# Expert lists visited in fixed blocks of 128 rows, with a short table for the rest

## What is computed

```python
scores = sigmoid(x @ gate_weight.T); sc = scores + gate_bias
# best 2 of 4 groups, then the best 6 of their experts
_, topidx = top_k(where(emask > 0, sc, -inf), 6)
tw = take_along_axis(scores, topidx); tw = tw / (tw.sum() + 1e-20) * 0.2
routed = sum over the 6 chosen e of tw[e] * (silu(x @ w_gate[e]) * (x @ w_up[e])) @ w_down[e]
anchor = the same with one of 16 smaller experts: topidx[:, 0] // 2
out = routed + shared + 0.1 * anchor
```

## Time and profile before

| | us |
|---|---|
| median of 3 runs (421.95 to 535.0) | 422.62 |
| span of the profiled execution | 412.1 |
| around the span, if that execution is like the median | 10.5 |
| last slots written | 178.8 |
| first visit's rows turned on TensorE | 203.14 |
| first routed up-product | 240.53 |

### The profile page before, as it was taken

The page is one execution under the profiler, slowest core; times in us unless marked ns, Lnnn a source line. Parts: engine busy times, 40 slices in busy tenths (PEclk is TensorE's granted clock), DMA queues, the critical chain, the costliest instruction groups (busy, mean ns, idle before and its releaser), DMA issues.

```text
span 412.1 us, 8817 instructions
## 1 busy us (share of the span) xinstructions
PE 343.3 (83%) x2552; PEld 299.1 (73%) x2552; DVE 278.0 (67%) x1171; ACT 190.0 (46%) x471; POOL 181.7 (44%) x159
## 2 busy tenths in 40 slices
PE   5999999999899968773889999999999999994000
PEld 3786978779687857561677789999999999993000
DVE  0466789989798886798357775555565665666675
ACT  1152153441545233400157777777877777771000
POOL 6000000588888768767871374344422344433000
PEclk9999999999999997985989999999999999998555
DMA  7999999986698643694555576555555559531998
GB/s 234 298 335 335 329 341 328 420 320 119 123 337 252 126 96 86 218 387 137 152 162 130 167 214 180 162 158 165 165 145 162 166 155 291 168 113 58 303 303 245
DMA packets 55823, 88.44 MB, mean 215 GB/s; under 512 B 16145, under 2 KB 46521, under 8 KB 55513
## 3 DMA queue, kind: packets, MB, share of 16 engines
q1 hardware_dynamic: 38192, 67.66, 52.9%
q0 software_dynamic: 16720, 19.48, 17.8%
q10 hardware_dynamic: 864, 0.73, 0.6%
HBM read 50.62 MB, written 37.09 MB: 213 GB/s over the span
## 4 chain that ended last, share of the span: by engine, by line
PE 60%; DVE 20%; DMA 8%; issue 3%; ACT 3%; SPq 3%; DVEq 2%; POOLq 0%
PE B L823 20%; PE B L838 10%; PE B L514 6%; PE B L812 5%; DMA W<-sums_d 4%; PE B L549 4%; PE B L632 3%; PE B L598 2%; PE B L618 2%; DVEq L319 2%; DMA e_sb<-rows_d 2%; SPq L419 2%; DVE ring L1589 1%; PE B L656 1%; DMA W<-in_pt 1%
## 5 line engine op out<-in xcount | busy, mean ns | idle before, releaser
L457 POOL DMA_INDIRECT rows_d<-spent,slot x77 | 104.1, 1352 | 97.3 <-issue 90.9
L823 PEld LDWEIGHTS B<-e_sb,UPW 128*128 128x128 f32 x796 | 105.4, 193 | 10.7 <-issue 5.5
L823 PE MATMUL B<-e_sb,UPW 128*128 128x128 f32 x796 | 108.9, 278 | 1.5 <-issue 1.5
L1597 DVE TENSOR_TENSOR e_sb<-e_sb,B 128x128 f32<-128x128 f32 (+1 forms) x112 | 32.3, 288 | 62.2 <-ACT e_sb L990 55.8
L981 ACT COPY UPW<-W 128x512 f32 (+1 forms) x112 | 63.9, 570 | 22.2 <-issue 13.9
L838 PE MATMUL B<-W,e_sb 128*128 x224 | 69.3, 391 | 0.8 <-DVE e_sb L1597 0.8
L483 POOL DMA_INDIRECT sums_d<-spent x32 | 31.1, 972 | 48.7 <-DVE spent L1589 47.9
L812 PE MATMUL B<-ident,e_sb 128*128 128x128 f32 x224 | 43.1, 274 | 1.9 <-DMA e_sb<-rows_d 1.8
L990 ACT ACTIVATE e_sb<-B 128x128 f32<-128x128 f32 (+1 forms) x112 | 30.9, 276 | 22.2 <-PE B L823 20.8
L514 PE MATMUL B<-W 128*111 128x256 f32 (+1 forms) x132 | 34.2, 406 | 4.6 <-DMA W<-in_pt 4.5
L483 POOL DMA_INDIRECT sums_d<-W,tok_full x24 | 23.2, 966 | 30.3 <-ACT W L995 29.7
(11 more groups left out here) (250 smaller groups left out, 524.0 us busy)
## 6 DMA issues: line engine op xcount, KB each, us to landing
e_sb<-rows_d SPq DMA_DIRECT2D x112, 161.0 KB, 2.3
rows_d<-spent SPq DMA_DIRECT2D x2, 7728.0 KB, 44.4
W<-in_wx SPq DMA_DIRECT2D x1, 6643.0 KB
W<-sums_d SPq DMA_DIRECT2D x13, 448.0 KB, 9.4
W<-in_wx SPq DMA_DIRECT2D x10, 516.5 KB, 9.5
W<-in_wx SPq DMA_DIRECT2D x1, 4576.0 KB, 18.7
W<-in_pt SPq DMA_DIRECT2D x4, 666.0 KB, 6.9
W<-sums_d SPq DMA_DIRECT2D x7, 336.0 KB, 11.1
```

Of the source, the lines that this page charges most:

```text
L457: pool.indirect_dma_start(rows_d, bass.IndirectOffsetOnAxis(ap=slot[0:n, t, j:j + 1], axis=0), xrow[0:n, t, :], None).then_inc(done, 16)
L823: mm = pe.matmul(B[2 + i % 2][:, m * P:(m + 1) * P], UPW[:, i % 2, at:at + P], GT[:, i % 2, k, :], start=k == 0, stop=k == KC - 1)
L1597: dve.tensor_tensor(out[0:n, i % 2, :], S[0:n, i % 2, :], ups, ALU.mult).then_inc(H_ok, 1)
```

## The change

There are again 112 visits, of four kinds: `a`, the first 128 rows of each of the 16 anchor lists; `b`, 9 further blocks of anchor lists; `r`, the first 128 rows of each of the 32 routed lists; `s`, 55 further blocks. For `a` and `r` the row offset, the weights and the weight column are constants, so nothing is read from the table and the gate and up weights are multiplied straight from `W`. For `b` and `s` a table of 64 places holds the weights' offset, the row and the column; a place without a block points to dummy rows. Further blocks are counted from a list's end, so only first blocks are partly filled; their unused rows go to spare rows of `sums_d` (`keep`, `spare`). No tile is summed in SBUF: each visit's weighted result goes to one of 22 buffers and is sent alone, 112 indirect DMAs; ScalarE weighs every second `a` visit, VectorE the others. All turned copies are ScalarE's. Only the first 128 rows of the lists are filled in advance. SP's queue and TensorE no longer wait for the table ahead of the first visit. At the end of the first part `route` comes ahead of `shared_down(2)`, `shared_down(3)` ahead of the table, `shared_mult(3)` ahead of the last `choose`; the product for the masks (`slot_bounds`) and some filler products (`stay_busy`) are gone.

```diff
--- before.py
+++ after.py
...
+ANCHOR_MORE = (TOKENS - 1) // P
+ROUTED_MORE = (TOKENS * TOPK - TOPK) // P
+KINDS = "a" * ANCHORS + "b" * ANCHOR_MORE + "r" * EXPERTS + "s" * ROUTED_MORE
 XT = len(KINDS)
 INDEX = [KINDS[:i].count(k) for i, k in enumerate(KINDS)]
-TILE_AXIS, EXTRA_AXIS = 1000, 2000
-RING = D + 1
+FIRST_ROUTED = ANCHORS + ANCHOR_MORE
+MORE = ANCHOR_MORE + ROUTED_MORE
+ROUTED_AXIS = 1000
 GB = 6
-PL = 3 * EXPERTS + ANCHORS
+NY, NY_OWN = 22, 10
...
+def weighed_by_act(i):
+    return KINDS[i] == "a" and i % 2 == 1
...
+        def up_place(i):
+
+            return ANCHOR_COLS + INDEX[i] * WX if routed(i) else INDEX[i] * ANCHOR_WX
+
+        def result(i):
+
+            u = i % NY
+            return Y_own[:, u * D:(u + 1) * D] if u < NY_OWN else spent[:, (u - NY_OWN) * D:(u - NY_OWN + 1) * D]
+
+        def free_result(engine, i):
+
+            if NY_OWN <= i < NY:
+                engine.wait_ge(hs_ok, NB)
+            if i >= NY:
+                engine.wait_ge(y_sent[i % NY], 16 * (i // NY))
...
-            for half in range(2):
-                sp.dma_start(of_list[half * P:(half + 1) * P, :, :],
-                             padrow[:, :].unsqueeze(1).to_broadcast([P, LISTS, ROW])).then_inc(empty, 16)
+            of_list = rows_d[P:P + LISTS * LIST_ROWS, :].rearrange("(l r) n -> r l n", r=LIST_ROWS)
+            sp.dma_start(of_list[0:P, :, :], padrow[:, :].unsqueeze(1).to_broadcast([P, LISTS, ROW])).then_inc(empty, 16)
...
             sp.wait_ge(scat_anchor, 16 * NT)
             sp.wait_ge(ini_d, 16 * 4)
-            sp.wait_ge(table_ok, 1)
             sp.wait_ge(av_ps, NT)
 
             def load_rows(i):
+                if i == ANCHORS:
+                    sp.wait_ge(table_ok, 1)
                 if i == FIRST_ROUTED:
                     sp.wait_ge(scat, 16 * NT * TOPK)
                 if i >= GB:
 
                     sp.wait_ge(T_ps, i - GB + 1)
                     sp.wait_ge(meta_ok, i - GB + 1)
-                row = entry(mybir.EngineType.SP, 1, i, DUMMY_ROW + P)
-                sp.dma_start(G[:, i % GB, :], rows_d[bass.ds(row, P), :]).then_inc(g_ld[i % GB], 16)
+                if looked_up(i):
+                    row = entry(mybir.EngineType.SP, 1, i, DUMMY_ROW + P)
+                    rows = rows_d[bass.ds(row, P), :]
+                else:
+                    row = P + (INDEX[i] + (0 if routed(i) else EXPERTS)) * LIST_ROWS
+                    rows = rows_d[row:row + P, :]
+                sp.dma_start(G[:, i % GB, :], rows).then_inc(g_ld[i % GB], 16)
...
                 if i == XT - 16:
-                    sp.wait_ge(sent_anchor, 16 * ANCHOR_PACKED)
-                    sp.wait_ge(sent_full, 16 * FULL)
+                    for u in range(NY):
+                        sp.wait_ge(y_sent[u], 16 * sends_of(u, FIRST_ROUTED))
                     load_part(TOPK)
             sp.wait_ge(D_ps, XT)
-            sp.wait_ge(sent_mixed, 16 * MIXED)
+            for u in range(NY):
+                sp.wait_ge(y_sent[u], 16 * sends_of(u, XT))
...
-            pool.wait_ge(hs_ok, NB)
-            pool.memset(spent[:, 0:until_scattered], 0.0).then_inc(mixed_zero, 1)
-            pool.wait_ge(scat_anchor, 16 * NT)
-            pool.wait_ge(scat, 16 * NT * TOPK)
             pool.wait_ge(ini_d, 16 * 4)
-            pool.memset(spent[:, until_scattered:MIXED * RING], 0.0).then_inc(mixed_zero, 1)
...
+            for i in range(XT):
+                pool.wait_ge(Y_by[weighed_by_act(i)], weighed_before(i) + 1)
+                pool.indirect_dma_start(sums_d, bass.IndirectOffsetOnAxis(ap=to_row[:, i:i + 1], axis=0),
+                                        result(i), None).then_inc(y_sent[i % NY], 16)
...
+            route(NB - 1)
             shared_down(2)
-            route(NB - 1)
             shared_up(4)
             rank(NB - 1)
-            stay_busy(12, 3, w_sgu)
+            shared_down(3)
+            stay_busy(9, 3, w_sgu)
             table_rows()
-            shared_down(3)
-            slot_bounds()
             shared_up(5)
             shared_down(4)
-            stay_busy(4, 3, w_sgu)
             shared_down(5)
...
-            pe.wait_ge(table_ok, 1)
-            pe.wait_ge(valid_ok, 1)
-            pe.wait_ge(hs_ok, NB - 2)
+            pe.wait_ge(slot_ok, NB)
+            pe.wait_ge(hs_ok, 3)
...
-                pe.wait_ge(gt_by[copied_by_act(i)], copies_before(i) + 1)
-                pe.wait_ge(upw_ok, i + 1)
+                if i == FIRST_ROUTED:
+                    pe.wait_ge(ld["late0"], 16)
+                    pe.wait_ge(ld["late1"], 16 * LATE_PIECES)
+                pe.wait_ge(gt_ok, i + 1)
+                if looked_up(i):
+                    pe.wait_ge(upw_ok, sum(looked_up(k) for k in range(i + 1)))
...
+                        if looked_up(i):
+                            gate_or_up = UPW[:, i % 2, at:at + P]
+                        else:
+                            gate_or_up = W[:, up_place(i) + at:up_place(i) + at + P]
+                        mm = pe.matmul(B[2 + i % 2][:, m * P:(m + 1) * P], gate_or_up, GT[:, i % 2, k, :],
...
-                if i + 2 == FIRST_ROUTED:
-                    act.wait_ge(ld["late0"], 16)
-                    act.wait_ge(ld["late1"], 16 * LATE_PIECES)
                 hidden_silu(i)
                 if i + 2 < XT:
-                    copy_up(i + 2)
-                    if copied_by_act(i + 2):
-                        turned_copy(i + 2)
-                if i >= 1 and KINDS[i - 1] == "F":
+                    if i + 2 == ANCHORS:
+                        act.wait_ge(ld["lists"], 16)
+                        act.wait_ge(table_ok, 1)
+                    if i + 2 == FIRST_ROUTED + EXPERTS:
+                        act.wait_ge(ld["late0"], 16)
+                        act.wait_ge(ld["late1"], 16 * LATE_PIECES)
+                    if looked_up(i + 2):
+                        copy_up(i + 2)
+                    turned_copy(i + 2)
+                if i >= 1 and weighed_by_act(i - 1):
                     weigh(i - 1)
...
             shared_mult(2)
+            dve.memset(H_anchor[:, :, :], 0.0).then_inc(half_zero, 1)
+            shared_mult(3)
             choose(NB - 1)
             place(NB - 1)
...
+            step(dve.scalar_tensor_tensor(whole[:, :], base[:, :], float(P - 2), base0, ALU.add, ALU.subtract))
+            step(dve.tensor_scalar(whole[:, :], whole[:, :], 7, None, ALU.logical_shift_right))
+            step(dve.tensor_scalar(more, whole[:, :], 1.0, -1.0, ALU.max, ALU.add))
+            dve.tensor_tensor_scan(ends[:, R], ones[:, 0:EXPERTS], more[:, R], float(ROUTED_AXIS), ALU.mult, ALU.add)
+            dve.tensor_tensor_scan(ends[:, A], ones[:, 0:ANCHORS], more[:, A], 0.0, ALU.mult, ALU.add)
+            step(dve.scalar_tensor_tensor(behind, more, -float(P), base[:, :], ALU.mult, ALU.add))
+            step(dve.tensor_tensor(starts, ends, more, ALU.subtract))
+            dve.tensor_scalar(mine, ends, number, None, ALU.is_gt)
+            step(dve.scalar_tensor_tensor(first_rows, starts, -float(P), behind, ALU.mult, ALU.add))
             step(dve.scalar_tensor_tensor(mine, starts, number, mine, ALU.is_le, ALU.mult))
...
+            dve.reduce_sum(unused_c, mine, axis=AX.X)
+            step(dve.tensor_tensor(picked, facts, mine.unsqueeze(1).to_broadcast([P, 3, LISTS]), ALU.mult))
+            dve.tensor_scalar(unused_c, unused_c, -1.0, 1.0, ALU.mult, ALU.add)
+            step(dve.reduce_sum(tcol[:, 0:3], picked, axis=AX.X))
+            dve.tensor_scalar(weight_c, weight_c, first_w, None, ALU.add)
+            dve.scalar_tensor_tensor(col_c, unused_c, dummy_col, col_c, ALU.mult, ALU.add)
+            step(dve.scalar_tensor_tensor(place_c, unused_c, dummy_row, row_of_number, ALU.mult, ALU.add))
+            dve.tensor_tensor(place_c, place_c, row_c, ALU.add).then_inc(cols_ok, 1)
+
+            step(dve.tensor_tensor(behind, behind, base0, ALU.subtract))
+            step(dve.tensor_scalar(keep, behind, pcol, None, ALU.is_gt))
+            step(dve.scalar_tensor_tensor(spare, keep, -1.0, spare_rows, ALU.mult, ALU.mult))
+            step(dve.tensor_tensor(spare, spare, spare_rows, ALU.add))
...
-                dve.tensor_tensor(wcol[:, i:i + 1], G[:, i % GB, bass.ds(at, 1)], mask, ALU.mult)
+                dve.tensor_copy(wcol[:, i:i + 1], G[:, i % GB, D:D + TO_ROW][:, bass.ds(at, 1)])
+                to = G[:, i % GB, D + TO_ROW:ROW][:, bass.ds(at, 1)]
+                if looked_up(i):
+                    dve.tensor_copy(to_row[:, i:i + 1], to).then_inc(meta_ok, 1)
...
+                    q = INDEX[i] + (0 if routed(i) else EXPERTS)
+                    dve.scalar_tensor_tensor(to_row[:, i:i + 1], to, keep[:, q:q + 1], spare[:, q:q + 1],
+                                             ALU.mult, ALU.add).then_inc(meta_ok, 1)
...
+                free_result(dve, i)
                 dve.wait_ge(D_ps, i + 1)
                 dve.wait_ge(meta_ok, i + 1)
-                if sums_before(i) > 0:
```

(16 more changed lines are left out.)

328 lines of the change are left out of this document (82 added, 246 removed).

## The result

| | before | after |
|---|---|---|
| median, us | 422.28 | 406.81 (404.53 to 408.18) |
| ratio, 95% interval | | 0.969, 0.962 to 0.976 |
| span of the profiled execution | 412.1 | 404.6 |
| its time around the span | not known | 406.38 − 404.6 = 1.8 |

The change is faster by 3.1%; the forecast was 410.8 us, −2.8%, with the range 402 to 417. The ratio counts undisturbed runs alone (one run of before took 535.0 us), so it is not the quotient of the two medians.

The account below looks back on a forecast made before the run. TensorE bounds the routed visits, VectorE's register loads the anchor visits, with a serial table-and-gather stretch ahead. First routed visit −13.1 (including first visit −9.1), routed ±0, end +1.3: −11.8, span 400.3, plus 10.5 around it: 410.8 us, range 402 to 417.

Parts of the forecast that it names:

- around the span: Time outside the profiled span: 10.5 us, if the profiled execution is like the median.
- last slots: Last slots written on VectorE: router products moved ahead of shared_down(2) bring them forward by 0.4 us, bounds 0 to 1.1.
- last slots to anchor rows landed: The last anchor scatter ahead of the first gathers needs 8.8 us to land, at 187.5.
- Table off the path: VectorE's table ahead of the visits: 13.7 us falls to 2.9, up to 4.5; the first 16 visits need no table.
- First gathers: SP's gathers ahead of the first visit: 6.4 us, bounds 2.5 and 9; first visit at 194.0, −9.1 us.
- the 197: Ahead of the first visit: the forecast is wrong if the first rows land later than 197.
- Neither 2.5 nor 10 us: Gather times of two rivals: fast gathers, 2.5 us, total 403, chance 17%; starved gathers, 10 us, total 415.2, chance 18%.
- Anchor visits and ramp: 25 anchor visits: 28.4 us plus 1.0 pipeline, 2.0 clock, 2.0 shared gathers; first routed visit at 227.4, −13.1 us.
- Routed visits: The 87 routed visits on TensorE stay at 1.54 us each: ±0.
- Sends: 112 GpSimd sends instead of 66, 1.28 us each, level with the results near i = 70: hidden.
- End: After the last visit: +1.6 for SP's 22 semaphore waits, −0.3 for dropped VectorE steps, together +1.3 us.
- VectorE blocked by the sends: Rival, chance 5%: sends stall VectorE's small copies in the visits, +15 us on 55 looked-up visits, total 426.

Follow-up runs that it names:

- experiment 1: The changed kernel unaltered, run again for a second profile: 405.32 us, ratio 0.965.
- experiment 7: The changed kernel with extra table reads in its 25 anchor visits, their values unused, so the same kernel in effect: 406.16 us, ratio 0.970.
- experiment 11: The changed kernel with 60 idle VectorE steps ahead of the table and no wait for it ahead of the first visit: 416.05 us, ratio 0.995.
- the second profile of before: The kernel before unaltered, run again: 420.22 us against 420.06, span 419.5.
- kernel 10: The changed kernel with 60 idle VectorE steps ahead of the table; SP and TensorE wait for it ahead of the first visit: 418.63 us, ratio 0.999.
- experiment 5: The changed kernel with five of ten late-weight pieces issued behind the gathers of visits 5 to 9: 409.67 us, ratio 0.976.

## Why the prediction was right, step by step

| step | forecast | three profiles of after (after, 1, 7) |
|---|---|---|
| last slots | 178.4 | 182.7, 180.2, 180.5 |
| last slots to anchor rows landed | 9.1 | 9.3 in after |
| last slots to first rows | 15.6 | 13.3, 13.9, 17.4 |
| first rows to first routed | 33.4 | 33.6, 34.1, 32.8 |
| routed visits | 135.1 | 136.7, 136.9, 136.9 |
| end | 37.8 | 38.3, 36.4, 35.9 |
| around the span | 10.5 | 1.8, 2.1, 1.8 |

*Table off the path.* VectorE's chain for it, first and last instruction, in after:

```profile
182.71 0.21 DVE L1418 SCALAR_TENSOR_TENSOR whole<-base,small 128x48 int32<-128x48 f32 x1
...
186.26 0.22 DVE L1435 TENSOR_TENSOR tcol<-tcol 128x1 f32<-128x1 f32 x1
```

3.8 us, inside the 2.9 to 4.5 of the prediction, against the 13.7 of the earlier trace rows. The step's result is right, its reason only half: the prediction had the first sixteen visits free of the table, but TensorE turns it ahead of them (experiment 11). TensorE's leftovers were done at 192.0 and covered nothing in after, as it said. In before they did count: they ended at 203.10, when the first visit began, so their shortening is part of what the prediction put down to the table and the gathers.

*First gathers.* The first took 3.8 us (SP's first issue at 192.03, TensorE's rows at 195.98), the second 5.75, the median until 212 was 6.6. In experiment 1 the first rows came 5.0 us behind SP's first issue (189.16 to 194.14), in experiment 7 7.3 (190.62 to 197.92). So the 6.4 taken was too long in two of three, and in the third the first rows came later than the 197 that the prediction had named as a sign of being wrong, with its slots 2.1 us later than forecast. Neither 2.5 nor 10 us came about; of the rows before, the 6.87 of the earlier trace rows was the one to go by.

*Anchor visits and ramp.* 1.10 a visit, and 1.12 in the mean for the looked-up ones, where 1.20 was taken; the rest, 33.6 − 27.7 = 5.9, is ramp: the pipeline, four microseconds at 0.50 of the clock, and stalls on gathers of 1.56, 0.65 and 0.73 us. The forecast had 28.4 + 5.0. For the clock 2.0 was taken; 4 us at 0.50 cost at most 2.0 and 12 at 0.92 at most another 1.0, less where TensorE was empty anyway.

*Routed visits.* 1.54 us unchanged, with one stall of 1.4 us that was not foreseen. The prediction looked at what the visits compute and did not follow the queue at the place where SP's wait went from two semaphores to 22.

*Sends.* GpSimd's timeline in after, the first send, the first that waited for its result alone, and the last:

```profile
212.73 0.98 POOL L492 DMA_INDIRECT sums_d<-Y_own,to_row  x1 [0.30 <-issue]
...
297.05 0.97 POOL L492 DMA_INDIRECT sums_d<-Y_own,to_row  x1 [0.56 <-DVE Y_own L1476]
...
367.44 1.45 POOL L492 DMA_INDIRECT sums_d<-Y_own,to_row  x1 [0.30 <-issue]
```

1.27 us each back to back, level with the results after 66 sends (212.73 + 1.27 × 66 = 296.6), where about 70 were forecast. The last send waits only for GpSimd's own cadence.

*End.* The term +1.6 was mis-sized: the waits for 22 semaphores hide behind the last send. The chain at the end:

```profile
367.44 2.88 DMA sums_d<-Y_own,to_row
370.32 0.02 SPq L439
...
370.44 0.34 SPq L429
...
377.54 19.58 DMA W<-sums_d
```

From the landing of the last send to the first part's load pass 0.12 us. The end's length varies from 35.9 to 39.6 us over both kernels, because the last load of the sums does: 19.58 us here, 17.74 and 17.11 in experiments 1 and 7, 17.57 and 20.61 in the two profiles of before. Without it the end is 18.6 to 18.8 us after and 18.9 and 19.0 before, so nothing was added there.

*VectorE blocked by the sends.* This rival falls. One-element copies over all 112 visits of after, and the scalar product out of PSUM in 57 of the 104 that VectorE weighs (the other 47 take 478 to 485), min, median and max in ns:

```profile
L1462 DVE COPY wcol<-e_sb x112: 142/146/155, 196.8 to 362.5; 128x1 f32 x64, 128x1 f32<-128x1 f32 x48
...
L1476 DVE TENSOR_SCALAR spent<-B,wcol x57: 472/484/485, 215.3 to 364.1; 128x256 f32<-128x256 f32 x57
```

*Size.* The one term that was far off is the 10.5 us around the span: each profiled execution with a known time has 1.8 to 2.1 us there. The rest of it was the difference between a quick execution (412.1) and the median. That did not touch the forecast, which is the median less 11.8, nor the terms: the second profile of before (419.5) is longer by 3.7 us up to the last slots and by 3.1 at the end, and by 0.6 in between. Of the terms, the way from the last slots to the first routed product shrank by 13.6 us where 12.7 were forecast. The stall of 1.4 to 1.7 us among the routed visits was not foreseen, and the 1.3 us charged to the end did not come; that these two nearly cancel is luck. Measured gains are 13.7 to 15.5 us. What they have above 11.8 is less than the sections of one kernel vary by, and is not placed further.

## What to carry to other kernels

An engine that looks busy all the time can still be held by another: the anchor visits were read off the chain, and one register load of 0.31 us, taken from a queue that had no room left, gave 1.5% by itself. To take a wait away gains nothing while another engine's own order keeps the same dependence; look for the instruction that produces the awaited value in every queue, and shorten its chain. A transfer that is moved out of the way of the path has to be put where the engines have room, or it costs more than it gave.

## What the runs showed of the hardware

The sixty idle steps (60 tensor_scalar instructions of 128 × 48 from SBUF to SBUF) took 297 ns on average. All of them (min, median and max in ns), then chain and timeline of kernel 10, VectorE and GpSimd:

```profile
L1420 DVE TENSOR_SCALAR idle<-base x60: 186/188/736, 182.0 to 201.1; 128x48 f32<-128x48 f32 x60
```

```profile
182.43 0.20 DVE idle L1420
...
182.87 0.75 DVE idle L1420
```

```profile
182.26 1.36 POOL L471 DMA_INDIRECT rows_d<-spent,slot  x1 [2.15 <-DVE slot L1244]
183.93 1.35 POOL L471 DMA_INDIRECT rows_d<-spent,slot  x1 [0.30 <-issue]
```

A step takes 0.20 us, except one in each scatter's period of 1.65 us, which takes 0.75 and ends with GpSimd's instruction (182.87 + 0.75 = 183.62 = 182.26 + 1.36). So a step that meets the end of a scatter stands still until it is over, while the step at 182.43 ran at full speed inside the same scatter. The mean fits: twelve scatters fall into the sixty steps, and 60 × (297 − 188) ns = 6.5 us is twelve times 0.55. The Trainium skill, page "SBUF — State Buffer", section "Who interferes with whom", has tensor_scalar and copies in a two-port mode and GpSimd contend: whichever issues first gets the shared ports for its whole instruction, and the other is blocked. The trace agrees for the SBUF tensor_scalar as to who is blocked, but not for the whole scatter: the price is 0.55 us of its 1.36. For the one-element copies of 112 visits and VectorE's 104 products out of PSUM no stall is to be seen.

The gathers' time to land goes with what else the DMA engines do: 3.8 to 8.1 us beside the dispatch (after, experiments 1 and 7), 3.4 in the median from 212 to 230, and 9 to 10 with the held weights on top (experiment 5).
